# Rotated attention in a two-layer decoder kernel: the order of all engines redrawn, the turned halves summed on GpSimd

## The reference

```
q = x @ wq + bq;  k = ctx @ wk + bk;  v = ctx @ wv + bv
q, k = rotate(q, pos), rotate(k, pos)      # pairs of features turned by pos * freq
s = (q k^T) / sqrt(8), causal              # per head, 64 x 64
p = softmax(s);  o = p v
out = layernorm(x + o @ wo + bo)
```

## Time and profile before

| | us |
|---|---|
| median of 3 runs | 6087.42 |
| lowest, highest | 6083.26, 6090.32 |
| the profiled execution, its own time | 6088.12 |
| its span, first to last instruction | 6086.5 |
| rotated stage in it, about | 2395 to 2800 |

### The profile page before, as it was taken

One profiled execution on the slowest core, in us unless ns is written; L12 is line 12 of the kernel. 1 busy time (PEld: TensorE's weight loads), 2 busy tenths in 40 slices (PEclk: granted clock), 3 DMA queues, 4 the chain that ended last, 5 costly groups with the idle time before them and its releaser, 6 DMA issues. The chain is left out here.

```text
span 6086.5 us, 171007 instructions
## 1 busy us (share of the span) xinstructions
PE 5034.2 (83%) x62308; PEld 2991.6 (49%) x62308; DVE 4753.2 (78%) x7971; ACT 3400.4 (56%) x5148; POOL 3326.9 (55%) x3129
## 2 busy tenths in 40 slices
PE   6999999999999976887867965999967758887990
PEld 3444444444444334665655633666645536666440
DVE  6999999999999985896865355777759949998334
ACT  4666666666666644556841211444447738887440
POOL 4444455444444314665734574555537738887674
PEclk9999999999999998998979977999989969999995
DMA  1111111112111113221123641000001111111443
GB/s 51 52 46 51 48 49 48 52 44 53 45 53 45 49 51 88 56 57 34 47 71 86 146 118 53 20 16 18 15 23 48 49 30 48 50 50 40 158 145 84
DMA packets 584082, 347.70 MB, mean 57 GB/s; under 512 B 63977, under 2 KB 562476, under 8 KB 583468
## 3 DMA queue, kind: packets, MB, share of 16 engines
q1 hardware_dynamic: 562268, 312.85, 18.1%
q0 software_dynamic: 11648, 21.26, 1.8%
q10 hardware_dynamic: 9552, 5.58, 0.3%
HBM read 180.39 MB, written 66.85 MB: 41 GB/s over the span
## 5 line engine op out<-in xcount | busy, mean ns | idle before, releaser
L1431 ACT ACTIVATE mb_dA<-ps,mb_a_neg 128x1024 f32<-128x1024 f32 x1008 | 1123.9, 1115 | 513.2 <-PE ps L1192 505.0
L1872 DVE TENSOR_TENSOR mb_m<-mb_dA,ps 128x704 f32<-128x704 f32 x1008 | 892.7, 886 | 31.5
L1879 DVE TENSOR_TENSOR ps<-mb_m,ps 128x704 f32<-128x704 f32 x992 | 882.0, 889 | 0.6
L1175 PE MATMUL ps<-mb_m,mb_ident 128*32 128x320 f32 x7936 | 740.8, 445 | 1.6
L1224 PE MATMUL ps<-mb_m,mb_cz 128*32 128x256 f32 x8064 | 621.2, 380 | 10.1 <-DVE mb_m L1872 6.2
L1866 DVE TENSOR_TENSOR mb_m<-mb_dA,ps 128x320 f32<-128x320 f32 x1008 | 484.2, 480 | 38.3 <-PE ps L1175 27.5
L1207 PE MATMUL ps<-mb_ur,mb_bl 64*128 64x256 bf16 x4032 | 388.2, 271 | 62.3 <-DVE mb_m L1872 59.4
L1192 PE MATMUL ps<-mb_ur,mb_sel 64*128 64x256 bf16 x4032 | 395.7, 275 | 15.2 <-ACT mb_dA L1431 10.8
L1224 PEld LDWEIGHTS ps<-mb_m,mb_cz 128*32 128x32 f32 x8064 | 259.5, 110 | 288.8 <-issue 10.8
L712 POOL TENSOR_TENSOR ea_p<-ea_p,ea_rec 128x2048 f32<-128x2048 f32 x70 | 253.5, 3622 | 89.6 <-DVE ea_rec L858 89.6
L1192 PEld LDWEIGHTS ps<-mb_ur,mb_sel 64*128 64x128 bf16 x4032 | 114.8, 94 | 376.2 <-issue 226.4
(11 more groups left out here) (507 smaller groups left out, 13275.0 us busy)
## 6 DMA issues: line engine op xcount, KB each, us to landing
mb_ur<-mb_pc SPq DMA_DIRECT2D x768, 64.0 KB
mb_bl<-mb_pc SPq DMA_DIRECT2D x576, 64.0 KB
ef_w<-in_ef_w SPq DMA_DIRECT2D x35, 515.5 KB
mx_w<-in_mx_w SPq DMA_DIRECT2D x39, 384.0 KB
moe_made<-mx_y SPq DMA_DIRECT2D x39, 256.0 KB, 2.4
ea_x<-hidden SPq DMA_DIRECT2D x280, 32.0 KB, 2.0
pairs<-ea_y SPq DMA_DIRECT2D x70, 128.0 KB, 1.9
ef_tk<-pairs SPq DMA_DIRECT2D x35, 256.0 KB
```

Of the source, the lines that this page charges most:

```text
L1175: mm = nc.tensor.matmul(out[c:c + 32], weights[:, c:c + 32], moving, start=start, stop=stop, skip_group_check=not grouped)
L1431: nc.scalar.activation(dA[:, t % RING].rearrange("p (g n) -> p g n", g=2), ps[:, DT:DT + 2, :], ACT.Exp, scale=a_neg[:, 0:1]).then_inc(dA_ ...
L1872: nc.vector.tensor_tensor(m[:, t % RING, DVE_PART], dA[:, t % RING, DVE_PART], state(u, t - 1, DVE_PART), ALU.mult).then_inc(md_ready.sem, 1)
L1879: nc.vector.tensor_tensor(h, m[:, t % RING, DVE_PART], h, ALU.add).then_inc(hd_ready.sem, 1)
```

## The change

Only the case with `rope` set changes. In each period: VectorE's list becomes times_cos(j+3), softmax_top(j+1), rotate(j+3), sums(j), finish(j-2), softmax_shift(j+1); add_turned moves to GpSimd, and is done for quad j+3 in period j, between add_bias(j+2) and normalise(j). GpSimd's tail_scale(j-2) goes from ahead of add_bias to behind normalise. TensorE's project_qk(j+3) goes ahead of scores(j+1). ScalarE's take_x(j+3) goes ahead of exponentials(j), and it scales quad j-3 instead of j-2, at the same place. There is one more period at the end (LAST).

```
--- before.py
+++ after.py
@@ -285,7 +285,7 @@
 
             return not isinstance(n, int) or 0 <= n < QUADS
 
-        FIRST, LO, HI, LAST = (-5 if pre_norm else -4), 4, QUADS - 8 if QUADS % 4 == 0 else QUADS // 4 * 4 - 4, QUADS + 1
+        FIRST, LO, HI, LAST = (-5 if pre_norm else -4), 4, QUADS - 8 if QUADS % 4 == 0 else QUADS // 4 * 4 - 4, QUADS + 1 + (rope is not None)
 
         def periods(eng, period):
 
@@ -534,10 +534,10 @@
 
                 def period(j, u):
                     one, three, past = (u + 1) % 4, (u + 3) % 4, (u - 1) % 4
+                    if rope and live(j + 3):
+                        project_qk(j + 3, three)
                     if mask is None and live(j + 1):
                         scores(j + 1, one)
-                    if rope and live(j + 3):
-                        project_qk(j + 3, three)
                     if live(j - 1):
                         turn_p(j - 1, past, 0)
                     if live(j + 3):
@@ -655,11 +655,11 @@
 
                 def period(j, u):
                     two, three, past = (u + 2) % 4, (u + 3) % 4, (u - 1) % 4
-                    if mask is not None and live(j + 3):
+                    if (rope or mask is not None) and live(j + 3):
                         take_x(j + 3, three)
                     if live(j):
                         exponentials(j, u)
-                    if mask is None and live(j + 3):
+                    if mask is None and not rope and live(j + 3):
                         take_x(j + 3, three)
                     if pre_norm and live(j + 4):
                         norm(j + 4, u)
@@ -669,7 +669,9 @@
                         square_means(j + 5, (u + 1) % 4)
                     if live(j + 3) and not rope:
                         take_qk(j + 3, three)
-                    if tail != "none" and mask is None and live(j - 2):
+                    if rope and live(j - 3):
+                        scale(j - 3, (u + 1) % 4)
+                    if tail != "none" and mask is None and not rope and live(j - 2):
                         scale(j - 2, two)
                     if live(j - 1):
                         take_p(j - 1, 1)
@@ -694,6 +696,14 @@
                     pool.wait_ge(nrstd_ready.sem, nrstd_ready.at(i, 1))
                     nc.gpsimd.tensor_tensor(nrstd[:], nrstd[:], half_neg[:], ALU.pow).then_inc(nrstd_ready.sem, 1)
 
+                def add_turned(i, u):
+
+                    pool.wait_ge(qs_taken.sem, qs_taken.at(i))
+                    pool.wait_ge(km_ready.sem, km_ready.at(i - 1))
+                    nc.gpsimd.tensor_tensor(kT[:], qc[:, 1], qs[:, 1], ALU.add).then_inc(rot_ready.sem, 1)
+                    pool.wait_ge(s_done.sem, s_done.at(i - 2))
+                    nc.gpsimd.tensor_tensor(qT[:, u % 2], qc[:, 0], qs[:, 0], ALU.add).then_inc(rot_ready.sem, 1)
+
                 def mask_heads(i, u):
 
                     pool.wait_ge(s_done.sem, s_done.at(i - 2))
@@ -742,7 +752,7 @@
                     if mask is not None and live(j + 1):
 
                         pool.wait_ge(s_masked.sem, s_masked.at(j + 1))
-                    if tail != "none" and live(j - 2):
+                    if tail != "none" and not rope and live(j - 2):
                         tail_scale(j - 2)
                     if pre_norm and live(j + 5):
                         norm_scale(j + 5)
@@ -750,8 +760,12 @@
                         add_bias(j + 2, two)
                     if mask is not None and live(j + 1):
                         subtract_top(j + 1, (u + 1) % 4)
+                    if rope and live(j + 3):
+                        add_turned(j + 3, (u + 3) % 4)
                     if live(j):
                         normalise(j, u)
+                    if rope and live(j - 2):
+                        tail_scale(j - 2)
 
                 nc.gpsimd.memset(half_neg[:], -0.5).then_inc(half_set.sem, 1)
                 nc.gpsimd.memset(eps[:], LN_EPS).then_inc(half_set.sem, 1)
@@ -801,14 +815,6 @@
                     for z, b in enumerate((bqs, bks)):
                         nc.vector.scalar_tensor_tensor(qs[:, z], lead_ps[:, 256 * z:256 * z + 256], b[:, 0:1], cs[:, u, 1],
                                                        ALU.add, ALU.mult).then_inc(qs_taken.sem, 1)
-
-                def add_turned(i, u):
-
-                    dve.wait_ge(qs_taken.sem, qs_taken.at(i))
-                    dve.wait_ge(km_ready.sem, km_ready.at(i - 1))
-                    nc.vector.tensor_tensor(kT[:], qc[:, 1], qs[:, 1], ALU.add).then_inc(rot_ready.sem, 1)
-                    dve.wait_ge(s_done.sem, s_done.at(i - 2))
-                    nc.vector.tensor_tensor(qT[:, u % 2], qc[:, 0], qs[:, 0], ALU.add).then_inc(rot_ready.sem, 1)
 
                 def mask_scores(i, u):
 
@@ -882,8 +888,6 @@
 
                 def period(j, u):
                     one, two, three = (u + 1) % 4, (u + 2) % 4, (u + 3) % 4
-                    if rope and live(j + 2):
-                        add_turned(j + 2, two)
                     if mask is not None and live(j + 1):
                         mask_scores(j + 1, one)
                     if mask is not None and live(j - 2):
@@ -892,20 +896,20 @@
                         mark_dead(j + 1, one)
                     if not rope and mask is None and live(j - 2):
                         finish(j - 2, two)
-                    if rope and live(j - 2):
-                        finish(j - 2, two)
+                    if rope and live(j + 3):
+                        times_cos(j + 3, three)
+                    if rope and live(j + 1):
+                        softmax_top(j + 1)
+                    if rope and live(j + 3):
+                        rotate(j + 3, three)
                     if mask is not None and live(j + 1):
                         softmax_shift(j + 1, one)
                     if not rope and mask is None and live(j + 1):
                         softmax_top(j + 1)
                     if live(j):
                         sums(j, u)
-                    if rope and live(j + 3):
-                        times_cos(j + 3, three)
-                    if rope and live(j + 1):
-                        softmax_top(j + 1)
-                    if rope and live(j + 3):
-                        rotate(j + 3, three)
+                    if rope and live(j - 2):
+                        finish(j - 2, two)
                     if mask is None and live(j + 1):
                         softmax_shift(j + 1, one)
```

More of the change, by code:

```diff
@@ L803, in rotate @@
                                                        ALU.add, ALU.mult).then_inc(qs_taken.sem, 1)
[L805 to L811, removed]
                 def mask_scores(i, u):
```

## The result

The changed kernel takes 6249.2 us in the median (6245.8 to 6260.7, 4 runs) against 6085.3 us (4 runs of the kernel before, the three of the section on the time before among them): ratio 1.027, 95% interval 1.0258 to 1.0283. The profiled execution has a span of 6244.1 us, 157.6 more than before.

The account below looks back on a forecast made before the run. VectorE bounded the rotated stage at 11.1 us a quad; a chain over all engines would make it 15.9. 26 quads gave +125, the last two intervals +9.6, filling +3, draining 0: +137, so 6224 us, range 6178 to 6262.

Parts of the forecast that it names:

- Part 1: VectorE and GpSimd: adds move, VectorE's own work falls to 9.74 us, but maxima wait for scores; alone 11.3 us a quad.
- Part 2: VectorE's residual add comes at 8.25 us and holds up TensorE's first value product, leaving TensorE idle over 4 us.
- Part 3: TensorE and ScalarE: copy of x and query product ahead of scores close the chain at a 14.5 us period.
- Part 4: TensorE's clock falls behind the gap, adding 1.4 us a quad (bounds 0.88 and 1.8): period 15.9 us.
- Part 5: Scaling a quad later on ScalarE, tail_scale last on GpSimd, later stores and one extra period: cost nothing.
- Filling: Start of the rotated stage: the query product delays the first scores, taken as +3 us (bounds 0 and +8).
- Draining: End of the rotated stage: the same chain of value products as before, so 0 us.
- (A): TensorE's clock stays at 1.00 in the rotated stage, +98 us: 6186 us; chance 0.16.
- (B): The wait for the residual add doesn't bind; GpSimd decides with a loop of 11.9 us: 6111 us; chance 0.06.
- (C): Only VectorE's wait for the naked scores costs, 11.3 us a quad: 6094 us, within 0.2%; chance 0.02.
- (D): VectorE stays the bound and what it sheds is gained, period 9.74 us: 6049 us; chance 0.04.
- (E): TensorE's lower clock lasts over the whole burst, some 3 us a period, 17.5 us: 6269 us; chance 0.09.

Follow-up runs that it names:

- e4: The changed kernel with the tail (finish) directly ahead of the sums on VectorE instead of directly behind: 6125.6 us, ratio 1.0061 to the kernel before.
- e2: The changed kernel with finish back at VectorE's front, tail_scale back ahead of add_bias and scaling back at quad j-2: 6078.0 us against 6086.1 before.
- e5: The changed kernel with 24 extra unread turnings of p filling TensorE's gap before the first value product: 6199.0 us, ratio 1.0186 to the kernel before.
- e6: The changed kernel with TensorE's scores(j+1) put back ahead of project_qk(j+3): 6262.4 us, ratio 1.0284 to the kernel before.
- e7: The kernel before with only the adds moved to GpSimd, for quad j+2 at its list's head: 6094.3 us against 6087.6, ratio 1.0003.
- e3: The kernel before with only the tail (finish) moved behind the sums, both still ahead of cosine product and maxima: 6124.3 us against 6087.6.

## Why the prediction was right, and where it was off

The forecast of 6224 us was low by 25, the measured 6249 inside the range of 6178 to 6262, and the sign and mechanism as stated. By its own steps:

- **Part 1.** VectorE's own work fell to 9.90 us (16.06 less 5.12 and 1.04 of idle time) for 9.74, and GpSimd's adds took 0.72 us for an estimate of 0.73. The maxima wait for naked scores: idle 1.04 us behind the cosine product. Right.
- **Part 2.** The residual add holds up TensorE's first value product: gap 4.37 us for 4.2, the same in every quad. e4, which moves only the tail, and e2 show that it is this place. Right.
- **Part 3.** The chain without the clock was put at 14.5 us; e5 has 14.54 outside its one pause. Right. The copy of x and the query product lie on it (0.39 us of idle, then 1.06 us to the scores), but e6 shows that the query product's place isn't a mistake by itself.
- **Part 4.** This term was mis-sized. Taken as 1.4 us (bounds 0.88 and 1.8), it measured 16.50 - 14.54 = 1.96, above its upper bound, and the period came to 16.50, not 15.9: 26 intervals x 5.4 = 140 us for 125. The statement that the first L523 hardly counts was the slip: at the lower clock it took 1.11 us instead of 0.69, and L470 was in most quads slow to its end. So shift to shift also missed the 15 to 16 us that were to show the forecast right, while the other signs came: L508 at 1.97, the clock below 0.95, add_bias waiting for the residual add. The rule of the Trainium skill that I had set beside it ("TensorE: Matmul & The Clock Gate", section "HAM oscillation — how this bites in real kernels"), that a kernel which waits too long at each step starts each burst at half clock, agrees with the trace in most quads: in 22 of 26 the first value product takes 1.10 us or more, in the other 4 it takes 0.69 or 0.70 and the clock falls in the turning behind it.
- **Part 5.** Filling was +3.2 us (shift 3 at 2471.38 instead of 2468.17) for +3, the last two intervals +10.0 (2900.33 to 2929.28 against 2756.88 to 2775.82) for +9.6. Draining was put at 0 and is +8.2: from the last shift to the start of the last scaling 29.2 us (2929.28 to 2958.47) instead of 21.0 (2775.82 to 2796.79). VectorE shows where:

```profile
2936.41 2.29 DVE L859 TENSOR_REDUCE x_total<-x_p 128x32 f32<-128x2048 f32 x1 [4.88 <-ACT x_p L630]
...
2948.66 0.42 DVE L880 TENSOR_TENSOR x_res<-ps,x_xr 128x256 f32<-128x256 f32 x1 [8.37 <-ACT x_y L653]
```

The last sums wait 4.88 us for exponentials that stand behind take_o in ScalarE's list, and the residual add of the last quad but one 8.37 us for the scaling of the quad before, which now comes a period later, a step that I had costed at nothing. With it the stage is 140 + 10 + 3 + 8 = 161 us longer; the profiled spans differ by 157.6 and the medians by 163.9.

Of the rivals, (A) is refuted by the clock of 0.83, (B) by the releaser of the gap, (C) and (D) by the time, and (E) lies 20 us above the result, no farther than the forecast lies below it. It had the first value product right and the rest of the burst wrong: the clock does recover before the turning of x (L439 and L531 at 0.44 and 0.71), and its period of 17.5 us is 1.0 too long where the forecast's 15.9 is 0.6 too short.

## What to carry to other kernels

Before a step is moved back in one engine's list, follow who waits for it on the others, and what stands in their lists behind that wait: here one add of 0.4 us, moved behind scores, maxima, sine products and sums, held up the value products and with them the whole of TensorE's list. Taking work off the busiest engine gains nothing while the step behind it waits for another one; the loop must be found first (e7). And a wait on TensorE can cost more than its length: 3.4 us of the new period was waiting, another 2.0 the clock, and filling the gap with useless turnings won 50 us back.

## What was not expected of the hardware

How much of a burst the lower clock takes: behind a gap of 4.37 us the value product went from 0.69 to as much as 1.11 us, the turning to 1.97 and project_v to 1.92, together 2.1 us if all three are hit. And the slowing is gone if the gap is cut into pieces of 0.24 and 1.29 us by unrelated turnings (e5).

The length of one gap doesn't tell by itself whether the clock falls. In e4 nothing changed behind 1.77 us, in any steady quad; in e3, where TensorE idles about 1.83 us in every quad, it fell in three of 26. In the masked stage of the kernel before, a gap of 2.74 us came ahead of a turning at full clock and a shorter one ahead of a slow one:

```profile
4610.48 1.09 PE L508 MATMUL ps<-x_ident,x_p 128*128 128x128 f32 x8 [2.74 <-POOL x_p L712]
...
4622.23 1.96 PE L508 MATMUL ps<-x_ident,x_p 128*128 128x128 f32 x8 [2.29 <-POOL x_p L712]
```

So a price of the clock taken from one or two rows, as in the prediction, is an estimate; how many quads pay it has to be counted.
